# One PSUM bank for all turned probabilities of the cross heads in a decoder layer on one Trainium2 core

## Chip, cores, metric

The kernel runs on one core of a Trainium2 chip. The metric is the device time of one execution in microseconds (us). The profile is one execution taken by the hardware profiler.

## What is computed

One decoder layer on x of 8 x 256 tokens x 256 channels, float32, with three blocks, each followed by a residual sum and a layer norm:

```
x = layernorm(x + self_attention(x))      # 16 heads, three branches mixed by a gate
x = layernorm(x + cross_attention(x, ctx))
x = layernorm(x + experts(x))             # 8 experts, 2 active, softmax over masked scores
```

The change is in the cross attention:

```
qm, km, vm = split_heads(q @ Wq.T + bq), split_heads(k @ Wk.T + bk), split_heads(v @ Wv.T + bv)
scores = einsum('bnlh,bnph->bnlp', qm, km) / sqrt(16)      # 16 heads of 16 channels, 256 x 256
scores = where(mask, scores, -1e8)
attn = softmax(scores, axis=-1)
out = einsum('bnlp,bnph->bnlh', attn, vm)                  # then merged and times Wo
```

## The kernel before

The attention stage works on the eight rows of the batch, one after another; the expert stage follows. Each engine has its own program, written out by hand, and semaphores tie them together. For a row i the order on every engine is: the last self heads of row i, the cross attention of row i (projections, then sixteen cross heads), and the first self heads of row i+1. Between these steps `interleave` (L154) puts the pieces of `front(i + 1)`, the projections, rotations and the selection of 64 keys of the next row, one piece after nearly each step. So a PE step of the cross heads is followed by products for the next row.

PSUM has eight banks: S0 to S3, T0, T1, O and X, each 128 partitions of 512 float32 numbers. `block_plan` (L170) lists in the order of the program which result goes to which bank. For each bank there is a pair of semaphores, full and free. `before(name, i)` is the count of the free semaphore at which the previous user of the bank has been read out, and PE waits for it ahead of the first write; `after` is the count once the result itself has been read out. If a result moves from one bank to another in the list, the waits on all engines move with it.

The cross heads, for rows 0 to 6, go by steps h = 0 to 19:

- PE (L1783 to L1840): in even steps the scores of heads h and h+1 (`scores_x`, to S0 and S1; products 32 rows deep, `ps_S<-kx_sb,qx_sb`, eight of them); then four transposes of the normalised probabilities of head h-3 (`turn_probs_x`, L1798 to L1806, `<-ident,pr`, L1804); in steps 7, 11, 15, 19 the products of four heads with the values (`values_x`, `ps_O<-pT_sb,vx`). In the last steps the first self heads of the next row come in.
- VectorE (L1358 to L1390): `scores_x` reads the scores of a head out of PSUM, adds the mask and keeps the maximum (L1365, two per head); `denominators` inverts the sums of the exponentials (L1246). In an even step it does scores h, denominators h-1, scores h+1, and only then `turn_probs_x`, the copy of a turned head out of PSUM (L1378), for the heads of `VECTOR_TURNS`: 1, 5, 9, 13, 14, 15.
- ScalarE (L939 to L970): the exponentials of head h (L946), and ahead of them in its step the copy of turned head h-3 (L958) for the other heads.
- POOL (L724): normalises the probabilities of head h-1 (L728), four slots in turn, and computes rotations for the next row (L668 to L678) in between.
- SP issues the moves of rotated queries and keys of the next row.

Before the change the turned probabilities of even heads 0 to 12 go to S0, between the scores of the even heads, and all others to T0. A wait of PE's holds back everything behind it in its program. The last row has a plan of its own (`late`): turned heads in T0 and T1 in turn, scores in four banks.

The functions `turn_probs_x` and `scores_x` on PE wait like this:

```
for h in (h0, h0 + 1):                                   # scores_x, even step
    turns, f, row_ = sx(i, h)
    pe.wait_ge(turns.free_sem(f), turns.before(f, row_))
pe.wait_ge(prob_sb.sem, prob_sb.at(i, NH + h + 1))       # turn_probs_x
pe.wait_ge(turns.free_sem(f), turns.before(f, row_))
```

Of the kernel before, what the change touches and what calls it, by code (L numbers as in the profile page):

```python
# [19 lines left out]
NH = 16  # L20
# [149 lines left out]
def block_plan(full, free):  # L170

    plan = BankPlan(full, free)
    for h in range(NH):
        for half in range(2):
            if h >= HEAD_START:
                plan.add(("s", h, half), f"S{2 * (h % 2) + half}")
        for half in range(2):
            plan.add(("pT", h, half), f"T{half}")
    for g in range(4):
        plan.add(("o", g), ("X", "O")[g % 2])  # L180
    plan.add("proj", "S0")
    plan.add("ctxT", "O")
    plan.add("kx", "S0")
    plan.add("vx", "S1")
    plan.add("x1T", "T0")
    plan.add("qx", "O")
    for k in range(NH + 3):
        if k < NH and k % 2 == 0:
            plan.add(("sx", k), "S0")
            plan.add(("sx", k + 1), "S1")  # L190
        if k >= 3:
            h = k - 3
            plan.add(("pxT", h), "S0" if h % 2 == 0 and k < NH else "T0")
    for g in range(2):
        plan.add(("ox", g), "O")
    plan.add("projx", "O")


    for n, name in enumerate((
# [5 lines left out]
        plan.add(name, FRONT_BANKS[n % len(FRONT_BANKS)], ahead=True)  # L205
    for n, name in enumerate((("ksT", 0), ("ksT", 1))):
        plan.add(name, ("X", "T1")[n % 2], ahead=True)
    for h in range(HEAD_START):
        for half in range(2):
            plan.add(("s", h, half), f"S{2 * (h % 2) + half}", ahead=True)  # L210
    return plan
# [81 lines left out]
def attention_stage(nc, outer, block, sh, w):  # L293

    ctx = ExitStack()
    with ctx:
# [6 lines left out]
        BANKS = ("S0", "S1", "S2", "S3", "T0", "T1", "O", "X")  # L303
        pst = {b: ctx.enter_context(nc.psum_tensor(f"ps_{b}", [P, 512], F32)) for b in BANKS}
        plan = block_plan({b: sem(f"full_{b}") for b in BANKS}, {b: sem(f"free_{b}") for b in BANKS})

        def ps(name):
# [2328 lines left out]
```

## Time and profile before

| | |
|---|---|
| median of 3 runs | 1662.67 us (1662.43 to 1663.26) |
| the profiled execution | 1661.11 us |
| its span, first to last instruction | 1659.4 us |
| mean granted TensorE clock | 0.982 |
| PE busy | 1598.6 us, 96% |
| VectorE, ScalarE, POOL busy | 68%, 64%, 63% |
| attention stage | the first 975 us or so |

The profile names an instruction by its line, engine, operation, and out<-in tiles. A line of the timeline has its start, its length, and, in square brackets, the idle time of the engine ahead of it with what ended it. PE's matmuls overlap: a matmul's length is from its start to its modelled end, and the next one starts before that end. Where several of one kind follow each other they are merged (x4).

### The profile page before, as it was taken

The page shows a single profiled execution, that of the slowest core. Times are in us where ns is not written, and L with a number is a line of the kernel's source. Part 1 is how long each engine was busy: PE and PEld are TensorE (multiplying, and loading weights), DVE is VectorE, ACT ScalarE, POOL GpSimd, SP SyncE. Part 2 cuts the span into 40 slices and gives each one's busy share as a digit, 9 for nine tenths or more (in the row PEclk, how much of TensorE's full clock was granted, in tenths as well). Part 3 has the DMA queues.
Part 4 walks back from the last instruction along what each step waited for, and adds up shares of the span by engine and source line. Part 5 has one row for each costly group of instructions (what it writes and reads, how often), then busy time and mean ns, then how long its engine had stood idle before and what let it go on. Part 6 is the DMA issues. An engine that isn't in the chain of part 4 may idle for free.

```text
span 1659.4 us, 31027 instructions
## 1 busy us (share of the span) xinstructions
PE 1598.6 (96%) x9793; PEld 1251.9 (75%) x9793; DVE 1126.3 (68%) x3867; ACT 1058.0 (64%) x3165; POOL 1041.8 (63%) x1514
## 2 busy tenths in 40 slices
PE   6899999999999999999999899999999999999997
PEld 5577686786776776776867668888888888888886
DVE  4668768776877776687678546656565656666567
ACT  1575866946948847758579664556565666665652
POOL 2465665846747746657558474667675757575753
PEclk9899999999999999999999999999999999999998
DMA  7203103013012021031030110010101010101001
GB/s 223 69 2 78 27 2 93 11 29 76 2 45 60 2 60 44 2 77 27 12 87 2 53 52 27 18 60 18 68 16 64 14 64 14 64 13 64 13 1 51
DMA packets 54899, 70.77 MB, mean 43 GB/s; under 512 B 12688, under 2 KB 40976, under 8 KB 54736
## 3 DMA queue, kind: packets, MB, share of 16 engines
q1 hardware_dynamic: 54016, 66.04, 13.9%
q10 hardware_dynamic: 720, 2.75, 0.5%
q8 instruction: 79, 1.29, 0.3%
q14 instruction: 84, 0.69, 0.1%
HBM read 37.23 MB, written 2.16 MB: 24 GB/s over the span
## 4 chain that ended last, share of the span: by engine, by line
PE 78%; POOL 6%; issue 5%; ACT 5%; DVE 5%; DVEq 0%; POOLq 0%; ACTq 0%
PE ps_Y L2397 21%; PE ps_H L2397 19%; PE ps_S L1455 18%; PE ps_O L1455 5%; PE ps_T L1684 5%; PE ps_X L1455 5%; ACT pr L892 5%; POOL pr L728 3%; PE ps_T L1455 2%; PE ps_T L1804 2%; POOL rot L668 1%; PE ps_S L1804 1%; DVE sm L1365 1%; POOL rot L678 1%; POOL rot L674 1%
## 5 line engine op out<-in xcount | busy, mean ns | idle before, releaser
L2092 POOL TENSOR_TENSOR h_lo<-h_sb,h_hi 128x512 fp32r<-128x512 f32 x256 | 337.1, 1337 | 207.7 <-ACT h_sb L2135 207.3
L693 POOL TENSOR_TENSOR pr<-pr,rden 128x128 f32<-128x128 f32 (+2 forms) x768 | 307.9, 437 | 84.2 <-DVE rden L1246 83.8
L892 ACT ACTIVATE pr<-sm,nmx 128x128 f32<-128x128 f32 (+2 forms) x768 | 311.7, 413 | 22.4 <-DVE nmx L1257 22.4
L2134 ACT ACTIVATE h_hi<-h_sb,b_sb 128x512 fp32r<-128x512 f32 x224 | 160.6, 717 | 183.1 <-DVE h_sb L2318 183.1
L2318 DVE TENSOR_TENSOR h_sb<-ps_H,part 128x512 f32<-128x512 f32 x168 | 115.6, 688 | 211.6 <-PE ps_H L2397 200.5
L728 POOL TENSOR_TENSOR pr<-pr,rden 128x256 f32<-128x256 f32 x256 | 151.0, 618 | 116.3 <-DVE rden L1246 116.0
L1257 DVE CUSTOM_DVE_ANT_0 sm<-ps_S,cmask 128x128 f32<-128x128 f32 (+2 forms) x768 | 192.6, 308 | 33.5 <-PE ps_S L1455 24.6
L2397 PE MATMUL ps_Y<-h_hi,w_hi 128*128 128x512 f32 x512 | 199.7, 390 | 0.0
L2397 PE MATMUL ps_Y<-h_hi,w_lo 128*128 128x512 f32 x512 | 199.2, 389 | 0.0
L2397 PE MATMUL ps_Y<-h_lo,w_hi 128*128 128x512 f32 x512 | 199.2, 389 | 0.0
L2135 ACT ACTIVATE h_sb<-h_sb,b_sb 128x512 f32<-128x512 f32 x224 | 158.9, 709 | 0.0
L946 ACT ACTIVATE pr<-sm,nmx 128x256 f32<-128x256 f32 x256 | 127.9, 502 | 47.7 <-DVE nmx L1365 47.5
L892 ACT ACTIVATION_READ_ACCUMULATOR pr<-sm,nmx 128x1 f32 x768 | 148.9, 194 | 0.0
L1365 DVE CUSTOM_DVE_ANT_0 sm<-ps_S,sm 128x256 f32<-128x256 f32 x256 | 96.6, 417 | 53.8 <-issue 38.1
L1455 PE MATMUL ps_S<-kT_sb,qT_sb 96*128 96x320 f32 (+1 forms) x512 | 133.0, 382 | 0.0
L1684 PE MATMUL ps_T<-ident,pr 128*128 128x128 f32 x896 | 120.7, 275 | 10.8 <-DVE rot L1273 3.5
L1455 PE MATMUL ps_S<-latT_sb,qT_sb 128*128 128x128 f32 (+1 forms) x512 | 129.3, 335 | 0.9 <-DVE kT_sb L1235 0.9
L1684 PEld LDWEIGHTS ps_T<-ident,pr 128*128 128x128 f32 x896 | 100.8, 140 | 37.2 <-issue 23.3
L2397 PEld LDWEIGHTS ps_Y<-h_hi,w_lo 128*128 128x128 f32 x512 | 96.1, 188 | 20.0
L2397 PEld LDWEIGHTS ps_Y<-h_hi,w_hi 128*128 128x128 f32 x512 | 96.1, 188 | 20.0
L2397 PEld LDWEIGHTS ps_Y<-h_lo,w_hi 128*128 128x128 f32 x512 | 96.1, 188 | 19.8
L1455 PEld LDWEIGHTS ps_S<-kT_sb,qT_sb 96*128 96x128 f32 x512 | 88.0, 192 | 21.0 <-issue 0.6
(304 smaller groups left out, 3634.9 us busy)
## 6 DMA issues: line engine op xcount, KB each, us to landing
qT_sb<-rot SPq DMA_DIRECT2D x256, 64.0 KB, 2.0
w_raw<-in_W SPq DMA_DIRECT2D x16, 1024.0 KB, 6.7
kT_sb<-rot SPq DMA_DIRECT2D x192, 64.0 KB, 2.0
share<-shares SPq DMA_DIRECT2D x16, 512.0 KB, 3.7
xin<-in_x SPq DMA_DIRECT2D x8, 256.0 KB, 2.7
cin<-in_ctx SPq DMA_DIRECT2D x8, 256.0 KB, 2.7
w_kw<-in_wink ACTq DMA_DIRECT2D x2, 768.0 KB, 5.7
w_ks<-in_selk SPq DMA_DIRECT2D x2, 768.0 KB, 5.5
```

Source lines behind the costliest of these rows:

```text
L693: last = pool.tensor_tensor(p_, p_, rden[:, h % 2, n:n + 1].to_broadcast([P, width]), ALU.mult)
L728: last = pool.tensor_tensor(p_, p_, rden[:, h % 2, q:q + 1].to_broadcast([P, T]), ALU.mult)
L892: last = act.activation(pr[:, h % PR_SLOTS, a:a + width], sm[:, h % 2, a:a + width], ACT.Exp, bias=nmx[:, h % 2, n:n + 1], scale=-1.0, acc ...
L946: last = act.activation(prx[:, h % PR_SLOTS, T * q:T * q + T], smx[:, h % 2, T * q:T * q + T], ACT.Exp, bias=nmx[:, h % 2, q:q + 1], scale ...
L1257: ins = dve.tensor_tensor_reduce(out=sm[:, h % 2, a:a + width], in0=ps(f)[:, off:off + width], in1=cmask[:, m:m + width], scale=-ATT_SCALE ...
L1455: return pe.matmul(out, lhsT, rhs, start=start, stop=stop)
L1684: last = pe.transpose(ps(f)[:, dst:dst + P], p[:, a:a + P], ident[:, :])
L2092: pool.tensor_tensor(h_lo[:, g % RING, k, :], h_sb[:, k, :], h_hi[:, g % RING, k, :].bitcast(F32), ALU.subtract).then_inc(low_sb, 1)
L2134: act.activation(h_hi[:, g % RING, k, :], src, ACT.Relu, bias=bias)
L2135: act.activation(h_sb[:, k, :], src, ACT.Relu, bias=bias).then_inc(rect_sb, 1)
L2318: dve.tensor_tensor(out_, a, b, ALU.add).then_inc(sum_out, 1)
L2397: return pe.matmul(out_, lhsT, rhs, start=start, stop=stop)
```

## The change

In rows 0 to 6 the turned probabilities of all sixteen cross heads go to bank T0. S0 and S1 hold, in this stretch, the scores alone. The number and order of instructions are as before on each engine; the semaphores and counts that they wait for and raise follow from the list.

```
@@ -190,7 +190,7 @@
             plan.add(("sx", k + 1), "S1")
         if k >= 3:
             h = k - 3
-            plan.add(("pxT", h), "S0" if h % 2 == 0 and k < NH else "T0")
+            plan.add(("pxT", h), "T0")
     for g in range(2):
         plan.add(("ox", g), "O")
     plan.add("projx", "O")
```

## Rows read from the trace of the kernel before

**Rows 1.** The page, busy time of each engine over the span.
```profile
PE 1598.6 (96%) x9793; PEld 1251.9 (75%) x9793; DVE 1126.3 (68%) x3867; ACT 1058.0 (64%) x3165; POOL 1041.8 (63%) x1514
```

**Rows 2.** Two batch rows: us, PE, PEld, DVE, ACT, POOL busy, PEclk, DMA share, GB/s.
```profile
369.34:486.96 117.62, 114.78 (x844) 86.47 (x843) 86.40 (x401) 81.24 (x313) 73.46 (x144) 0.97 0.15 38
486.96:601.32 114.36, 111.53 (x843) 84.54 (x842) 86.48 (x401) 81.04 (x313) 73.55 (x144) 1.00 0.16 39
```

**Rows 3.** Same view, the same blocks of a long and of a short row.
```profile
394.50:401.30 6.80, 6.80 (x42) 4.71 (x41) 1.89 (x11) 3.79 (x12) 3.52 (x6) 0.50 0.40 96
512.20:519.00 6.80, 6.80 (x58) 4.00 (x56) 4.33 (x22) 5.29 (x17) 4.68 (x8) 1.00 0.34 82
```

**Rows 4.** Timeline of PE in the cross heads of row 3.
```profile
498.80 0.60 PE L1804 MATMUL ps_S<-ident,pr 128*128 128x128 f32 x4
499.23 1.89 PE L1455 MATMUL ps_S<-latT_sb,w_qd 96*128 96x256 f32 x8
501.27 1.13 PE L1455 MATMUL ps_S<-kx_sb,qx_sb 32*128 32x256 f32 x8
502.34 0.66 PE L1804 MATMUL ps_T<-ident,pr 128*128 128x128 f32 x4
503.64 0.66 PE L1804 MATMUL ps_S<-ident,pr 128*128 128x128 f32 x4 [0.65 <-POOL pr L728]
...
506.20 1.03 PE L1455 MATMUL ps_T<-latT_sb,w_qd 96*128 96x256 f32 x4
507.15 1.13 PE L1455 MATMUL ps_S<-kx_sb,qx_sb 32*128 32x256 f32 x8
...
509.38 0.63 PE L1804 MATMUL ps_S<-ident,pr 128*128 128x128 f32 x4
...
511.99 0.66 PE L1804 MATMUL ps_T<-ident,pr 128*128 128x128 f32 x4
...
513.42 0.66 PE L1804 MATMUL ps_S<-ident,pr 128*128 128x128 f32 x4
...
516.66 1.94 PE L1455 MATMUL ps_S<-w_ks,lat 128*64 128x512 f32 x8
...
523.21 0.63 PE L1804 MATMUL ps_S<-ident,pr 128*128 128x128 f32 x4 [0.51 <-DVE nmx L1365]
523.87 1.07 PE L1455 MATMUL ps_O<-pT_sb,vx 128*32 128x256 f32 x16
...
524.97 0.62 PE L1511 MATMUL ps_X<-ident,rot 64*96 64x64 f32 x8
525.70 0.62 PE L1511 MATMUL ps_T<-ident,rot 64*96 64x64 f32 x8
526.75 0.66 PE L1804 MATMUL ps_T<-ident,pr 128*128 128x128 f32 x4 [0.43 <-POOL pr L728]
527.26 0.46 PE L1455 MATMUL ps_S<-latT_sb,qT_sb 128*128 128x128 f32 x2
```

**Rows 5.** Timeline of VectorE (DVE) in the same heads.
```profile
499.29 0.68 DVE L1378 COPY pT_sb<-ps_T 128x512 f32<-128x512 f32 x1
...
508.46 0.42 DVE L1365 CUSTOM_DVE_ANT_0 sm<-ps_S,sm 128x256 f32<-128x256 f32 x1 [1.92 <-issue]
...
509.90 0.69 DVE L1378 COPY pT_sb<-ps_T 128x512 f32<-128x512 f32 x1
...
522.98 0.08 DVE L1365 DVE_READ_ACCUMULATOR2_ANT nmx<- 128x1 f32 x1
...
526.36 0.69 DVE L1235 COPY kT_sb<-ps_T 96x512 f32<-96x512 f32 x1 [1.32 <-PE ps_T L1511]
```

**Rows 6.** Timeline of ScalarE (ACT), copies of turned heads 3 and 11.
```profile
503.03 0.59 ACT L958 COPY pT_sb<-ps_T 128x512 f32<-128x512 f32 x1 [0.87 <-PE ps_T L1804]
...
523.14 0.59 ACT L958 COPY pT_sb<-ps_T 128x512 f32<-128x512 f32 x1
```

**Rows 7.** Timeline of POOL, normalisations of the last cross heads.
```profile
525.51 3.47 POOL L728 TENSOR_TENSOR pr<-pr,rden 128x256 f32<-128x256 f32 x6
```

More of the change, by code:

```diff
@@ L192, in block_plan @@
             h = k - 3
-            plan.add(("pxT", h), "S0" if h % 2 == 0 and k < NH else "T0")
+            plan.add(("pxT", h), "T0")
     for g in range(2):
```

## Prediction

> **What bounds the kernel.** Read first the busy times [rows 1]: PE is busy for 96% of the span, every other engine for at most 68%. A busy PE is not PE at its peak, so the next view is the stretch of one row of the batch, measured from its first cross scores to those of the next row [rows 2]. There are two kinds: 117.62 us and 114.36 us. The batch rows starting at 137.16, 369.34 and 601.32 are of the long kind, those at 254.82, 486.96 and 718.76 of the short (each within 0.2 us of the row shown). The clock view [rows 3] tells them apart: in three rows the clock granted to TensorE is 0.50, that is 1.2 GHz, for 6.8 us, while the same blocks run at 1.00, 2.4 GHz, in the other four. The price of one such drop is 117.62 - 114.36 = 3.26 us here; the other two pairs give a little less, and I take 3.1.
>
> The third view is PE in order of time inside the cross heads of a short row [rows 4]. Here the reader should look at start times: PE takes its blocks in program order, and the next block nearly always starts where the last one's array time ends (four transposes: 499.23 - 498.80 = 0.43 us). So PE's order is the path, and what counts is where a block starts later than that. A line with ps_S and x4 from L1804 is an even head's turned probabilities. By the program there are seven in each of seven rows (heads 0 to 12), and these 49 blocks are what the change moves.
>
> **What the change does, and what it removes.** Same instructions, same durations; only which release each of these blocks waits for changes. (1) Scores of heads k, k+1 no longer wait until ScalarE has copied head k-4's probabilities out of S0. (2) The probabilities of even head h no longer wait for VectorE's reading of score h+2. Both sound large; the array shows what they were. The scores of heads 6 and 7 start at 501.27, after eight products from 499.23. Four such products take 0.86 us (506.20 to 507.15 with the usual 0.09 of entry to the next scores), so eight end at 500.96 and the idle is 0.31, of which 0.22 is the wait for S0. The other scores of the row start within 0.1 us of the end of the block ahead, or behind a narrow product whose own tail is 0.2 to 0.3. Gain: **0.22 us a row**, at least 0 and, if all such tails were waits, at most 0.7.
>
> **What it adds.** Head h's four transposes now wait until head h-1 has been copied out of T0. I take 0.15 us from the end of a copy to the first transpose, because the read-out of the scores that ended at 523.06 [rows 5] released the transposes of 523.21 [rows 4]; 0.05 and 0.25 as ends. Working through the short row, heads in order:
>
> Head 2: VectorE copies head 1 only after the scores of heads 4 and 5, at 499.29 for 0.68 [rows 5]. Head 2 can start at 499.29 + 0.68 + 0.15 = 500.12 in place of 498.80: +1.32. VectorE was working without a break there, so its copy does not move. The scores of heads 6 and 7 then start at 500.12 + 0.43 + 1.73 + 0.09 = 502.37: +1.10, and head 3 at 503.44.
>
> Head 4: it waited for POOL at 503.64, and now for ScalarE's copy of head 3. That copy starts 503.03 - 502.34 = 0.69 after the first transpose and takes 0.59 [rows 6]: 503.44 + 0.69 + 0.59 + 0.15 = 504.87, a lag of 1.23.
>
> Head 6: scores 8 and 9 and VectorE behind them lag 1.23 (VectorE had been waiting for them: it starts on them at 508.46 [rows 5], after PE's 507.15). Its copy of head 5 comes behind both scores again: 509.90 + 1.23 + 0.69 + 0.15 = 511.97 against 509.38. Lag 2.59.
>
> Head 8: 511.99 + 2.59 + 0.69 + 0.59 + 0.15 = 516.01 against 513.42. Lag 2.59, and all up to the selected keys' products at 516.66 carries it.
>
> Head 12: ScalarE's copy of head 11 ends at 523.14 + 0.59 = 523.73 [rows 6], so head 12 starts at 523.88 in place of 523.21, 0.67 more (head 10 adds a little at most and I leave it out). Not all survives: head 13 at 526.75 waits for POOL, whose work runs on from the rotated selected keys into the next normalisations at 525.51 [rows 7], and this follows the lag of 516.66 only. But the two groups of selected keys are turned 1.10 and 1.83 us after the values' products (524.97 and 525.70 against 523.87), and VectorE's copy of the second (526.36, [rows 5]) releases the next row's first scores at 527.26. Both distances hold a wait for POOL, whose time doesn't move with head 12, so part of the 0.67 goes into it: I estimate that 0.26 does and 0.41 stays (ends 0 and 0.67).
>
> Sum per row 2.59 + 0.41 = **3.0 us**, seven rows 21.0. By the ends of the 0.15 (in four steps) and of the 0.41 a row costs 2.2 to 3.7. Heads 13 to 15 were in T0 before; the last row keeps its own plan; the expert stage and every DMA are untouched, at nothing. SP issues the same moves in the same order, released by POOL and ScalarE; PE asks for them only ahead of the next row's scores, and with PE later they have more time. POOL's queue and ScalarE's keep their order; behind ScalarE's later copy of head 2 stand only exponentials that wait for scores which lag as much.
>
> **The clock.** Ahead of each of the three drops stand the same blocks: head 5, three position products one column wide, head 6, a product 32 rows deep, scores 32 rows deep, head 7 (around 509.38 [rows 4]; the drops [rows 3]). Four rows pass this place at full clock, three do not, so it is at the edge. The change puts 1.36 us more idle into just this place. I expect the drop in all seven: four more, 4 x 3.1 = 12.4 us. The ends are three drops fewer and, since the idle before head 2 is new too, seven more.
>
> The Trainium skill (TensorE: Matmul & The Clock Gate, "A second HAM failure mode: psum-queue depth-cycling") says that short idles of PE between groups, from cycling through PSUM banks, can make the clock swing between its two levels; the trace agrees that this place swings, and by that rule the 12.4 stands.
>
> Profiled execution: 1661.11 (span 1659.4 and 1.7 around it). 1661.11 + 21.0 + 12.4 = 1694.5. The median of the runs is 1.56 above the profiled one: **1696 us**.
>
> The starts in [rows 4] also say that separating scores from probabilities frees hardly any array time, because front products of the next row already cover it. The Trainium skill (Perfetto Trace Analysis, "Optimizing Tensor Performance", Matmuls) wants independent groups to rotate through different PSUM banks, so that one's evacuation overlaps the next group. It speaks against this change, which takes the second bank from the transposes, and for it in what it does to the scores; the rows above price the first at 3.2 a row, the second at 0.22. By the rule alone there would be a loss without a size.
>
> **Rivals.** (a) Waits as worked out, clock as before: 1662.67 + 21.0 = 1684. For it: four rows do pass that place at full clock, and the drops may hang on the moment rather than on the idle. Chance 0.20. (b) More drops: the idle before head 2 or around head 12 brings a second one to each row, up to 7 x 3.1 more: 1706 to 1718. Against it: those places have wide products close by. 0.08. (c) One of the two long waits is hidden, because VectorE gets to head 1 or 5 sooner when its neighbours lag: 7 x 1.3 = 9 less than forecast or than (a), 1672 to 1687. 0.09. (d) Both are hidden, POOL's normalisation sets the pace, no change: 1660 to 1666. VectorE's copies would have to end 1.3 us earlier, and the first [rows 5] has no idle ahead of it. 0.08. (e) **Faster.** Mechanism: S0 free of copies lets scores go out early, so VectorE, waiting for the scores of head 8 (1.92 us idle ahead of 508.46 [rows 5]), runs ahead and finishes head h-1's copy before PE wants T0. Price: 0.22 at the scores, 0.22 before head 12, 7 x 0.44 = 3.1, and the three clock drops saved, 9.3: 1650. It decides at head 2: VectorE must be done with head 1 by 498.65; it is done at 499.97, held by its own work and not by scores. 0.05.
>
> **Numbers.** Forecast 0.50. The range leaves out (d), (e), half of (b) and a little of (c): 1676 to 1709. A measurement of this kernel can tell about 0.2% (3.3 us) from no change. Faster 0.05, same 0.08, slower 0.87.
>
> **What would show it.** In the profile after: ps_T with all 512 turned blocks' records of cross heads, none to ps_S; PE idle before even heads put down to VectorE's copy (line 1378) some 14 times with about 1.3 us, and to ScalarE's (line 958) at heads 4, 8 and 12; head 2 starts 0.15 us after the end of VectorE's copy of head 1, in place of 1.17 us before it. Rows 117.5 us without a drop and 120.6 with one; clock 0.50 in seven stretches. The forecast is wrong if head 2 still starts ahead of that copy's end, if rows of the short kind stay at 114.4, or if the waits are there and the clock drops in three rows or fewer.

## The result and the profile after

The changed kernel takes 1698.99 us (median of 4 runs, 1698.08 to 1703.56) beside 1662.55 for the kernel before in the same comparison (4 runs, 1655.21 to 1663.26). The ratio is 1.0259, with an interval of 1.0229 to 1.0289: slower by 2.6%. The forecast was 1696 and its range 1676 to 1709. The profiled execution took 1699.47 us, its span is 1697.8, the mean granted clock 0.971; before they were 1661.11, 1659.4 and 0.982.

The page of the changed kernel, busy times and the two slice lines of PE:

```profile
PE 1615.4 (95%) x9793; PEld 1261.5 (74%) x9793; DVE 1126.2 (66%) x3867; ACT 1060.7 (62%) x3165; POOL 1042.4 (61%) x1514
...
PE   6899999998998999999999989999999999999997
PEclk9899999998999998999998999999999999999998
```

Beside [rows 1]: the busy times of VectorE, ScalarE and POOL are within 3 us, and PE's grew by 17 us with the same 9793 instructions. An instruction count that stands still while busy time grows points to the clock; the rest of the 38.4 us by which the span grew must be idle. The same windows as [rows 2], for six rows of the batch, and then the longest and two common clock drops, a drop being a stretch at 0.50 (columns: us, PE, PEld, DVE, ACT, POOL busy, PEclk, DMA share, GB/s):

```profile
137.92:259.89 121.97, 116.30 (x843) 87.31 (x842) 86.38 (x401) 81.55 (x313) 73.58 (x144) 0.96 0.14 35
259.89:380.06 120.17, 114.54 (x843) 86.52 (x842) 86.54 (x401) 81.36 (x313) 73.61 (x144) 0.97 0.15 37
380.06:502.05 121.99, 116.35 (x844) 87.45 (x843) 86.44 (x401) 81.59 (x313) 73.58 (x144) 0.96 0.15 37
502.05:622.19 120.14, 114.52 (x843) 86.55 (x843) 86.53 (x401) 81.45 (x313) 73.58 (x144) 0.97 0.15 37
622.19:743.92 121.73, 116.01 (x843) 87.28 (x842) 86.55 (x401) 81.60 (x313) 73.66 (x144) 0.96 0.15 36
743.92:864.19 120.27, 114.38 (x843) 86.37 (x842) 86.70 (x401) 81.47 (x313) 73.55 (x144) 0.97 0.15 37
...
890.30:904.00 13.70, 13.70 (x63) 7.71 (x59) 4.27 (x22) 7.00 (x22) 4.74 (x8) 0.50 0.30 74
405.60:415.80 10.20, 10.20 (x51) 6.89 (x52) 2.50 (x14) 5.78 (x17) 3.64 (x7) 0.50 0.40 98
528.50:535.30 6.80, 6.80 (x39) 4.77 (x35) 1.98 (x11) 4.13 (x14) 3.46 (x6) 0.50 0.38 91
```

No row has a clock of 1.00 any more. Every row of the seven has a drop at heads 5 to 7, 6.8 us long in four, 10.2 in two and 13.7 in the seventh (864.19 to 980.89, 116.7 us beside 107.8 before); the fifth row has a second one of 3.4, at 665.0. That is 64.7 us at 0.50 beside 3 x 6.8 = 20.4 before.

The timeline of PE in row 3, which begins at 502.05 here and at 486.96 before, so that 15.09 is to be taken off for a comparison with [rows 4]:

```profile
513.02 1.03 PE L1455 MATMUL ps_T<-latT_sb,w_qd 96*128 96x256 f32 x4
515.20 0.63 PE L1804 MATMUL ps_T<-ident,pr 128*128 128x128 f32 x4 [1.14 <-DVE pT_sb L1378]
515.66 1.89 PE L1455 MATMUL ps_S<-latT_sb,w_qd 96*128 96x256 f32 x8
517.48 1.13 PE L1455 MATMUL ps_S<-kx_sb,qx_sb 32*128 32x256 f32 x8
518.54 0.66 PE L1804 MATMUL ps_T<-ident,pr 128*128 128x128 f32 x4
519.97 0.63 PE L1804 MATMUL ps_T<-ident,pr 128*128 128x128 f32 x4 [0.77 <-ACT pT_sb L958]
...
524.51 0.66 PE L1804 MATMUL ps_T<-ident,pr 128*128 128x128 f32 x4
...
525.37 0.36 PE L1455 MATMUL ps_S<-marks,upper 128*128 128x1 f32 x2
527.03 0.63 PE L1804 MATMUL ps_T<-ident,pr 128*128 128x128 f32 x4 [1.30 <-DVE pT_sb L1378]
527.59 0.69 PE L1455 MATMUL ps_S<-w_qd,latT_sb 32*128 32x512 f32 x1
...
530.42 1.12 PE L1804 MATMUL ps_T<-ident,pr 128*128 128x128 f32 x4
```

The two copies of VectorE that these waits name, and, from the list of the line of the transposes, its count and the waits ahead of it:

```profile
514.37 0.68 DVE L1378 COPY pT_sb<-ps_T 128x512 f32<-128x512 f32 x1
...
526.19 0.69 DVE L1378 COPY pT_sb<-ps_T 128x512 f32<-128x512 f32 x1
```

```profile
L1804 PE MATMUL ps_T<-ident,pr x512: 271/273/476, 144.2 to 1014.2; 128*128 128x128 f32 x171
...
  DVE pT_sb L1378: 17.1, 14
  ACT pT_sb L958: 13.5, 14
```

514.37 + 0.68 + 0.15 = 515.20: PE stands with head 2 until VectorE has copied head 1. 526.19 + 0.69 + 0.15 = 527.03: the same at head 6 behind the copy of head 5. Seven rows give 14 waits of 1.2 us on average (longest 1.3) on VectorE, and 14 of 1.0 (longest 1.2) on ScalarE, at heads 4 and 12. Neither kind was there before. In this row the clock falls at 528.5, behind the one-column products, the wait, head 6 and the product 32 rows deep: at 530.42 four transposes span 1.12 us, where the usual is 0.66.

### The profile page after: what moved, and what is told of

Same layout as the page of the kernel before. It is cut to its first block, busy times and chain, and to the rows that moved or that the text cites. A ratio compares the mean times of both kernels' runs of the same rounds, so it can differ in the third digit from the quotient of the medians.

```text
span 1697.8 us, 31027 instructions
## 1 busy us (share of the span) xinstructions
PE 1615.4 (95%) x9793; PEld 1261.5 (74%) x9793; DVE 1126.2 (66%) x3867; ACT 1060.7 (62%) x3165; POOL 1042.4 (61%) x1514
## 3 DMA queue, kind: packets, MB, share of 16 engines
q1 hardware_dynamic: 54016, 66.04, 13.7%
## 4 chain that ended last, share of the span: by engine, by line
PE 80%; ACT 6%; issue 6%; DVE 5%; POOL 3%; DMA 0%; DVEq 0%; POOLq 0%; ACTq 0%
PE ps_Y L2397 21%; PE ps_S L1455 20%; PE ps_H L2397 18%; ACT pr L892 5%; PE ps_O L1455 5%; PE ps_T L1684 4%; PE ps_X L1455 4%; PE ps_T L1804 3%; PE ps_T L1455 3%; POOL pr L728 1%; DVE sm L1365 1%; DVE pT_sb L1378 1%; DVE rt L1083 1%; POOL rot L678 1%; POOL rot L668 1%
## 5 line engine op out<-in xcount | busy, mean ns | idle before, releaser
L1684 PE MATMUL ps_T<-ident,pr 128*128 128x128 f32 x896 | 120.6, 274 | 10.8 <-DVE rot L1273 3.5
L1684 PEld LDWEIGHTS ps_T<-ident,pr 128*128 128x128 f32 x896 | 100.9, 140 | 37.2 <-issue 23.4
L1804 PE MATMUL ps_T<-ident,pr 128*128 128x128 f32 x512 | 89.1, 302 | 34.6 <-DVE pT_sb L1378 17.1
L1804 PEld LDWEIGHTS ps_T<-ident,pr 128*128 128x128 f32 x512 | 61.5, 153 | 75.1 <-issue 42.6
```

The lines of the kernel that those rows point to most:

```text
L1684: last = pe.transpose(ps(f)[:, dst:dst + P], p[:, a:a + P], ident[:, :])
L1804: last = pe.transpose(pst[turns.bank(f)][:, T * k + P * q:T * k + P * q + P], prx[:, h % PR_SLOTS, T * q + P * k:T * q + P * k + P], ident ...
```

## The experiments

The theory had two parts: waits of PE at heads 2, 6 (VectorE), 4 and 12 (ScalarE), and a clock drop that the wait at head 6 brings about. The experiments take these apart. Their ratios are to the kernel before in runs beside them (1658.3, 1658.9, 1657.2 and 1654.8 us in the four groups of runs, each between 1649.9 and 1665.8).

**Half of the change each.** First, only heads 2 and 6 go to T0, then only the other five (both edits are against the changed kernel):

```
-            plan.add(("pxT", h), "T0")
+            plan.add(("pxT", h), "S0" if h % 2 == 0 and k < NH and h not in (2, 6) else "T0")
```

> Of the even heads only 2 and 6 go to T0, the five others stay in S0. Theory (PE waits for VectorE's copies of heads 1 and 5, which stand behind two heads' scores, and the longer idle makes the clock drop in every row): the two waits of 1.3 us each remain, less 0.22 for the freed scores and a little that head 4 absorbs, 2.3 us a row or 16, and the clock falls in all seven rows, 12 to 17 more: 1690 us, range 1684 to 1696. Rival (the loss lies in the one bank as such, spread over all seven heads): two sevenths of 36 us, 1673.

```
-            plan.add(("pxT", h), "T0")
+            plan.add(("pxT", h), "S0" if h in (2, 6) else "T0")
```

> The reverse: heads 2 and 6 stay in S0, the five others go to T0. Theory: head 4 costs 0.13, head 10 0.13, head 12 0.67 of which 0.4 stays, the rest nothing: 0.6 us a row or 4, and the clock falls in three rows as before: 1667 us, range 1660 to 1672, so that the two halves of the change don't share the loss evenly. Rival (one bank as such): five sevenths of 36 us, 1689.

Two heads: 1693.13 us, ratio 1.0208 (1.0175 to 1.0241). Five heads: 1661.17 us, 1.0022 (0.9999 to 1.0045). The row with the shortest drop in the first, and the first row of the second kernel, which has none (the same windows):

```profile
499.04:617.16 118.12, 113.14 (x844) 86.00 (x843) 86.48 (x401) 81.34 (x313) 73.63 (x144) 0.99 0.15 37
```

```profile
137.99:252.94 114.95, 111.57 (x843) 84.34 (x842) 86.29 (x401) 81.03 (x313) 73.51 (x144) 1.00 0.15 37
```

Two of the seven moved heads carry nearly the whole loss, and they are those behind VectorE's copies. The other five cost some 0.4 us a row (rows without a drop take 114.75 to 114.95, in the kernel before 114.4 to 114.5). In the first kernel the clock is at 0.50 for 54.4 us of the seven rows, in the second for 10.2. So it is the waits at heads 2 and 6 that bring the further drops; no run here has one of the two without the other at its full length and the blocks around it unchanged, so the part of the wait at head 6 alone is argued from where the clock falls.

**The copy in between.** In the changed kernel, VectorE takes the copies of heads 1, 5 and 9 between the two scores of its step instead of behind both; every head stays in T0:

```
+                    ahead = following is not None and h - 3 in (1, 5, 9)
+                    if ahead:
+                        turn_probs_x(h - 3)
                     if h < NH and h % 2 == 0:
                         scores_x(h + 1)
-                    if 3 <= h < NH + 3:
+                    if 3 <= h < NH + 3 and not ahead:
```

> The changed kernel with VectorE's copies of turned heads 1, 5 and 9 put ahead of the second head's scores in its step, no longer behind both. Theory (the wait is VectorE's copy standing behind the scores): heads 2 and 6 start 0.7 us sooner each, 1.4 us a row; a row without a drop of the clock comes to 115.9 us (114.4 in the kernel before, 117.3 in the changed one), and with some drops left 1680 us, range 1670 to 1688. Rival (the copy follows the transposes whatever its place, or scores read later cost as much as is won): rows as changed, 1695 or more.

1682.83 us, 1.015 (1.012 to 1.018). Its one row without a drop, and PE at heads 2, 4 and 6 of that row:

```profile
376.18:491.93 115.75, 111.53 (x845) 84.59 (x844) 86.45 (x401) 81.14 (x313) 73.57 (x144) 1.00 0.15 39
```

```profile
388.63 0.63 PE L1807 MATMUL ps_T<-ident,pr 128*128 128x128 f32 x4 [0.46 <-DVE pT_sb L1378]
...
393.40 0.63 PE L1807 MATMUL ps_T<-ident,pr 128*128 128x128 f32 x4 [0.77 <-ACT pT_sb L958]
...
399.78 0.63 PE L1807 MATMUL ps_T<-ident,pr 128*128 128x128 f32 x4 [0.61 <-DVE pT_sb L1378]
```

The waits at heads 2 and 6 shrink by 0.68 and 0.69 us, a head's reading of scores on VectorE, and the wait at head 4 stays: what PE waits for is the place of the copy in VectorE's order. The drops stay in the other six rows (47.6 us).

**ScalarE copies heads 1 and 5.** The changed kernel with one list altered:

```
-VECTOR_TURNS = (1, 5, 9, 13, 14, 15)
+VECTOR_TURNS = (9, 13, 14, 15)
```

> The changed kernel with the copies of turned heads 1 and 5 given to ScalarE, which idles there; all heads still in T0. Theory (the loss is who copies, and behind what, not the one bank): head 2 doesn't wait, head 6 by 0.3 us, head 12 as in the changed kernel; a row without a drop 115.0 us, 1662 us in all, range 1655 to 1668, no more drops than in the kernel before. Rival (one bank for neighbouring heads costs a full hand-over of 1.4 us each time): 1680 or more.

1661.77 us, 1.0021 (1.0002 to 1.004). A row without a drop, and PE at heads 2 and 4 in it:

```profile
252.65:367.65 115.00, 111.45 (x844) 84.58 (x843) 84.97 (x399) 82.20 (x315) 73.47 (x144) 1.00 0.16 39
```

```profile
264.49 0.60 PE L1804 MATMUL ps_T<-ident,pr 128*128 128x128 f32 x4
...
269.31 0.66 PE L1804 MATMUL ps_T<-ident,pr 128*128 128x128 f32 x4 [0.84 <-POOL pr L728]
```

Head 2 has no idle ahead of it, head 4 waits for POOL as before, and head 6 still waits 0.20 us for ScalarE, in place of 1.30 for VectorE. With all heads in one bank a row costs 0.4 to 0.5 us over before, and the ratio falls from 1.0259 to 1.0021: the bank alone is nearly free, the release behind VectorE's queue is not. The kernel before with the same two copies on ScalarE was not run, so what the lighter VectorE gives by itself is not taken apart.

**The clock by itself.** The product behind head 6 is 32 rows deep. It is made 128 rows deep, in the changed kernel and in the one before, with the same columns. The product then multiplies by query weights as well, so that its values are not those of the layer: these two kernels serve for timing alone.

```
-                    product(i, ("v1", t), P, HW, [latT[QK:P, 1, P * t:P * t + P]], [w_dv[QK:P, :]])
+                    low = 0 if t == 0 else QK
+                    product(i, ("v1", t), P, HW, [latT[low:P, 1, P * t:P * t + P]], [w_dv[low:P, :]])
```

> The changed kernel with the first latent value product of each row run over all 128 rows of the array in place of 32, in the same time (it then multiplies by query weights as well, so these values are others than the reference's). No wait differs. Theory (the drops of the clock come from the little work that the array does around head 6): the granted clock stays at full there in most rows and the drops' share goes, 1699 - 25 = 1674 us, range 1670 to 1682; what stays above the kernel before with the same edit is the waits alone, 21 us. Rival (the longer rows have another cause, and the clock only goes with it, or falls for other reasons): 1697 or more.

> The kernel before with the same edit of the first latent value product (its values are others than the reference's). Theory: no drop of the clock in the seven rows, three times 3.1 us less: 1653 us, range 1651 to 1656. Rival: 1662, drops in three rows as before.

The changed kernel with it: 1683.52 us, 1.0147 (1.012 to 1.0174), a little more than its range allowed. The kernel before with it: 1651.53 us, 0.9965 (0.9944 to 0.9986), as expected. From head 6 to the scores behind the product it takes the same time at full clock, 1.55 us with the shallow product (kernel before) and 1.54 with the deep one:

```profile
391.75 0.63 PE L1804 MATMUL ps_S<-ident,pr 128*128 128x128 f32 x4
392.30 1.12 PE L1455 MATMUL ps_S<-w_qd,latT_sb 32*128 32x512 f32 x2
393.30 1.13 PE L1455 MATMUL ps_S<-kx_sb,qx_sb 32*128 32x256 f32 x8
```

```profile
389.10 0.63 PE L1805 MATMUL ps_S<-ident,pr 128*128 128x128 f32 x4
389.56 1.02 PE L1455 MATMUL ps_S<-w_qd,latT_sb 128*128 128x512 f32 x2
390.64 1.13 PE L1455 MATMUL ps_S<-kx_sb,qx_sb 32*128 32x256 f32 x8
```

Two rows of the changed kernel with the deep product and two of the kernel before with it:

```profile
137.18:254.46 117.28, 111.61 (x844) 84.14 (x843) 86.29 (x401) 81.24 (x313) 73.62 (x144) 1.00 0.15 36
491.95:609.01 117.06, 111.44 (x844) 84.25 (x844) 86.45 (x401) 81.24 (x313) 73.58 (x144) 1.00 0.15 38
```

```profile
137.59:252.21 114.62, 111.67 (x843) 84.42 (x842) 86.38 (x401) 81.06 (x313) 73.51 (x144) 1.00 0.15 37
...
481.26:595.60 114.34, 111.47 (x844) 84.53 (x843) 86.52 (x401) 81.06 (x313) 73.52 (x144) 1.00 0.16 39
```

This gives the waits a price free of the clock. Three rows of each kernel can be put side by side: 117.28 - 114.62, 117.06 - 114.34 and 117.22 - 114.52 are 2.66, 2.72 and 2.70 us. It also shows the drop to be a matter of its own: in the kernel before, with one deeper product, none of the seven rows has one. That is the profiled execution; of the others the mean granted clock speaks, .988 to .991 in all nine runs, while ten of the 18 of the kernel before beside them lie below .988. In the changed kernel, with its idle ahead of head 6, it is not enough: three rows still drop there (at 279.7, 634.7 and 873.6), and three short drops come in elsewhere, 27.2 us together beside 64.7. At 3.1 us for 6.8 that is some 12 us, more than the miss. Its row at 491.95 shows the end of the chain of waits too:

```profile
529.54 0.66 PE L1805 MATMUL ps_T<-ident,pr 128*128 128x128 f32 x4
531.36 0.63 PE L1805 MATMUL ps_T<-ident,pr 128*128 128x128 f32 x4 [1.16 <-ACT pT_sb L958]
```

From head 11 to head 12 it is 1.82 us; before it was 523.21 - 522.05 = 1.16 us in row 3.

**More work at the drop.** In the kernel before, two products of 128 rows and 256 columns fill the place ahead of the shallow one; in a second kernel head 1 is copied by ScalarE too, and head 2 is in T0:

```
+                    if t == 0:
+                        pe.wait_ge(plan.free_sem(("v1", t)), plan.before(("v1", t), i))
+                        for _ in range(2):
+                            mm(ps(("v1", t))[:, 0:T], ident[:, :], latT[:, 1, :])
...
-VECTOR_TURNS = (1, 5, 9, 13, 14, 15)
+VECTOR_TURNS = (5, 9, 13, 14, 15)
...
-            plan.add(("pxT", h), "S0" if h % 2 == 0 and k < NH else "T0")
+            plan.add(("pxT", h), "S0" if h % 2 == 0 and k < NH and h != 2 else "T0")
```

> The kernel before with two more products, 128 rows deep and 256 columns wide, into the bank of the first latent value product ahead of it, whose own first product overwrites them: the output is unchanged, PE has 0.43 us more work a row. Theory (the array's little work there makes the clock drop): no drops in the seven rows, rows of 114.9 us, 1654 us with a small spread, against 1650 to 1663 of the kernel before. Rival (added work is only added, drops stay): 1661 with the same spread.

> The same, and ScalarE copies head 1, with head 2 in T0, so that the scores of heads 6 and 7 no longer wait for S0. Theory: 0.2 us a row less than without it, 1652.5 us. Rival: the earlier copy delays ScalarE's exponentials and nothing is won, 1654 or more.

1657.52 us, 0.9993 (0.9975 to 1.0011), and 1658.06 us, 0.9996 (0.998 to 1.0012), where 1654 and 1652.5 were expected. The drops did leave the seven rows of both profiled executions. But a row takes 115.0 to 115.4 us instead of 114.4, 0.3 more than I had reckoned for the two products, and the last row, which has none of these products in it, has a drop of 23.9 us in the first kernel's trace, where the kernel before has one of 13.7. The second kernel wins nothing further: with S0 free the scores of heads 6 and 7 come 0.2 us sooner, but head 4 then waits 0.88 us for POOL instead of 0.65. Filling the place with added work costs what it saves; the deeper product costs no time.

**Full products between heads 5 and 6.** PE's piece with the last two query products (96 rows deep, 256 columns, 1.7 us) changes places with the one-column position products. So the query products now stand between heads 5 and 6 and the position products go ahead of the scores of heads 8 and 9, while the product 32 rows deep stays where it was, behind head 6; ScalarE's readings move by a piece. Its core, on PE, in the kernel before, the changed one, and the changed one with ScalarE's copies:

```
-                queries(1, 0)
-                queries(1, 3)
-                yield
...
+                yield
+
+                queries(1, 0)
+                queries(1, 3)
```

> The kernel before with two pieces of the next row's projections exchanged on PE (the last two query products, 1.7 us at full depth, come after head 5 and the three position products ahead of them; ScalarE's copies of them move along). Theory: the array works hard just where it had little to do, the clock stays at full in the seven rows, rows of 114.4 us, 1651 us with a small spread. Rival: ScalarE's later copies hold up its exponentials and POOL, PE waits for head 8, rows 1 us longer, 1657 or more.

> The changed kernel with the same exchange. Theory (PE's wait for T0 at head 6 is idle because nothing stands between heads 5 and 6; work there covers it, and head 2's wait stays): the wait at head 6 falls from 1.36 to 0.3 us, a row without a drop 116.2 us, and with a few drops left at other places 1667 us, range 1661 to 1676. Rival (the waits only move on): 1690 or more.

> The exchange together with all heads in T0 and ScalarE copying heads 1 and 5. Theory: no long wait and no drop, rows of 114.9 us, 1654 us with a small spread: one bank costs next to nothing once neither copy nor clock stands against it. Rival: ScalarE, with two copies more and the moved ones, becomes late, 1660 or more.

On the kernel before 1654.96 us, 0.9991 (0.9974 to 1.0008); on the changed one 1669.99, 1.0089 (1.0058 to 1.0119); with ScalarE's copies 1660.36, 1.0026 (1.0006 to 1.0047). A row of the second, and PE at head 6 in the next row:

```profile
257.91:373.89 115.98, 111.47 (x843) 84.49 (x842) 86.89 (x401) 81.09 (x313) 73.57 (x144) 1.00 0.16 39
```

```profile
395.79 1.03 PE L1455 MATMUL ps_X<-latT_sb,w_qd 96*128 96x256 f32 x4
396.65 1.03 PE L1455 MATMUL ps_T<-latT_sb,w_qd 96*128 96x256 f32 x4
397.81 0.63 PE L1804 MATMUL ps_T<-ident,pr 128*128 128x128 f32 x4
398.36 0.69 PE L1455 MATMUL ps_S<-w_qd,latT_sb 32*128 32x512 f32 x1
```

The second has the whole change in it, its wait at head 2 too, and no drop in any of the seven rows of its profiled execution. It takes 29 us less than the changed kernel, 7 of them by shorter waits (seven times 2.7 less 1.7), the rest by the clock. That execution was its fastest (1666.22 us, clock .989); the other three are at 1669.7 to 1670.6 and .985 to .987, so their rows may not all have been free of drops. Now eight products of known length (four ahead of 396.65, four behind it, 0.86 us each) stand ahead of head 6 and not three narrow ones: the idle there is 397.81 - 396.65 - 0.86 = 0.30 us where it was 1.30, so a row costs 1.7 over the 114.4 of the first kernel. The exchange changes two things at once, this idle and the blocks beside it; in the first kernel, which had no such idle, the blocks alone do it. That one missed its expected 1651 us though its rows were as expected, because the exchange in the ramp before the first row brings a drop of 13.7 us there (the first cross scores come at 140.5, before at 137.2). The third missed its 1654 as well: drops appear at 179.1, 756.0 and 872.0, none of which I foresaw.

**The exchange in the later rows alone.** The same exchange on the kernel before, for all rows but the first, whose products stand in the ramp (PE's side of it):

```
-                queries(1, 0)
-                queries(1, 3)
-                yield
+                if i == 0:
+                    queries(1, 0)
+                    queries(1, 3)
+                    yield
...
+                if i:
+                    queries(1, 0)
+                    queries(1, 3)
+                    yield
```

> The kernel before with the exchange in the seven interleaved fronts only, the first front (which nothing is interleaved with) as it was. Theory: e9's first cross scores came at 140.5 us in place of 137.2, because a drop of the clock in the first front lasted longer; with that front as before the 3.3 us are won back: rows of 114.4 us and 1651.5 us, at most 1654, faster than the kernel before by 0.3 to 0.5%. Rival: the first stage's drops vary from run to run by themselves, 1655 as e9.

1652.74 us (1650.53 to 1656.92, 12 runs), 0.998 (0.9962 to 0.9998): within the expected time, but 0.2% faster and not 0.3 to 0.5%, and that only just clear of no change. Two of its rows:

```profile
252.36:366.64 114.28, 111.35 (x843) 84.68 (x842) 86.75 (x401) 80.89 (x313) 73.50 (x144) 1.00 0.16 39
481.02:595.34 114.32, 111.38 (x843) 84.56 (x842) 86.73 (x401) 80.86 (x313) 73.50 (x144) 1.00 0.16 39
```

The first six rows have no drop (114.2 to 114.6 us); the seventh has one of 3.4. The kernel before took 1651.64 to 1665.76 in the 17 runs beside it, so that the fastest runs of the two differ by 1 us and the slowest by 9: what is won is mostly that the long times are missing.

## Why the prediction was right

It was right in direction, mechanism and range, 3 us short of the median. Part of that closeness is luck: against the profiled execution the waits were 2.1 us too large and the clock's term 7.8 too small, and the 1.56 us from the profiled time to the median was added on, where the changed kernel's median lies 0.5 below. The 3 drops of the kernel before were taken as given, too; its later runs spread from 1649.9 to 1665.8 us.

- **The gain** of S0 free of copies. The scores of heads 6 and 7 start at 517.48 - 15.09 = 502.39, the forecast was 502.37. From the eight products ahead of them it is 517.48 - 515.66 = 1.82 us and was 501.27 - 499.23 = 2.04: the 0.22 of the working.
- **Head 2** starts at 515.20 - 15.09 = 500.11, forecast 500.12. **Head 4**: 519.97 - 15.09 = 504.88, forecast 504.87. **Head 6**: 527.03 - 15.09 = 511.94, forecast 511.97. The 0.15 us from a copy's end to the first transpose, taken from one place of the trace, held at both copies of VectorE. ScalarE's waits show at heads 4 and 12, 14 times; the one foretold for head 8 is there by the start times (head 8 comes 1.42 us after head 7, 520.84 - 519.42 in the row at 491.95), but the profile puts no idle to it.
- **Head 12** waits 0.66 us longer than before from head 11, forecast 0.67.
- **The sum of the waits** was 3.0 us a row and measured 2.7, so 7 x 2.7 = 18.9 and not 21.0. Two things were mis-sized. The lag of head 6 is as forecast (2.56 for 2.59), but it was taken to reach the selected keys whole, and there it is 2.40: their products start 524.05 - 491.95 = 32.10 us after the row's first scores (changed kernel with the deep product), before 516.66 - 486.96 = 29.70. From head 6 to head 7 it takes 519.42 - 516.93 = 2.49 us, before 511.99 - 509.38 = 2.61. And of head 12's 0.67, 0.41 was to stay: the first products of the next self heads start at 534.95 - 491.95 = 43.00 us after the row's first scores, before at 527.26 - 486.96 = 40.30, so 2.70 - 2.40 = 0.30 stays.
- **The clock.** Forecast: a drop in all seven rows, 3.1 us each, so four more, 12.4 us. There is one in all seven rows at the place named, but three of them are longer than any seen there before, and the fifth row has a second one. 64.7 - 20.4 = 44.3 us more at half clock, at 3.1 us for 6.8, are 20.2 us. This is the term that was too small: the number of drops was counted and their length taken for granted. Rows of 120.6 us were forecast; three are within 0.5 of that, three are 1.1 to 1.4 above it, and the seventh is 8.9 above its own former 107.8, where 6.1 was forecast.
- **The sum** then reads, against the profiled spans: 18.9 + 20.2, plus 0.8 ahead of the first row and less 1.4 behind the last row's first scores, 38.5; measured 1697.8 - 1659.4 = 38.4.

The rivals. (a) Waits with the clock as before, 1684: the waits were right, the clock was not. (b) A second drop in each row: one row has one. For the rest the time beyond the forecast comes from longer drops, which (b) did not name; its 1706 was not reached. (c) and (d), one or both waits hidden: both stand, 14 times. (e), faster through an early copy: head 2 is released at 514.37 + 0.68, after PE wants it, as the working said; VectorE was held by its own work.

On the Trainium skill (TensorE: Matmul & The Clock Gate, "A second HAM failure mode: psum-queue depth-cycling"): the place did swing as that rule says of short idles between groups. But idle is not the whole of it here: the kernel before, with no idle added and one deep product, lost its drops. On the Trainium skill (Perfetto Trace Analysis, "Optimizing Tensor Performance", Matmuls): the rule to rotate banks pointed the right way for the change, though with ScalarE's copies a single bank costs 0.4 to 0.5 us a row and not 2.7.

What stays open is why the drops are of 6.8 us in one row and 10.2 or 13.7 in another with the same blocks in it. The traces show one regularity: in the first six rows of the changed kernel the drops that start 25.4 and 25.6 us after the row's first scores last 10.2, those that start at 25.8 to 26.9 last 6.8 (the second, short one of the fifth row apart); with heads 2 and 6 alone in T0, 10.2 belongs to starts at 24.5 to 25.8, 6.8 to 26.0 to 26.9 and 3.4 to 27.3. What sets the start is not shown. The new places of the kernels with ScalarE's copies are not scattered either: four of their five drops start 37.0 to 37.3 us after the row's first scores, where head 12 (at 36.9 to 37.1) now waits 1.2 us for ScalarE, which is the place that rival (b) named. That this wait brings them on was not tested.

## What to carry to other kernels

Before a result is moved to a bank, look at who empties the bank's previous result and what stands ahead of that copy in its engine's order: a copy behind two heads' readings of scores cost PE 1.1 to 1.3 us each time, the same copy on another engine nothing at head 2 and 0.2 at head 6. Where a trace shows the clock falling at one place in some rows and not in others, count that place as fragile, and price idle put there at a whole drop in every row, or more: 64.7 us of drops came of 20.4 here. First try another order of the pieces: full products between the narrow ones cost nothing in a row here (114.2 to 114.6 us) and steadied the times from run to run. Added work cost what it saved. A deeper product cost no time, but the two kernels that had one computed other values; whether rows of zeros would do the same was not run.

## What the runs showed of the hardware

The depth of one product can go with whether the clock falls. In the kernel before, making the one product behind head 6 128 rows deep in place of 32, at the same columns, took the drops out of all seven rows, 1651.5 us for 1658.3. It is not this depth alone: with the product left 32 rows deep at its place, and query products put between heads 5 and 6 where the one-column products had stood, the seven rows of the profiled execution had no drop either. Where 1.3 us of idle stands ahead of head 6, as in the changed kernel, the depth alone took out a little over half of the drop time (27.2 us left of 64.7); the exchange, which also cuts this idle to 0.3, took out all of it in the profiled execution. The Trainium skill (TensorE: Matmul & The Clock Gate, "What's actually happening") says that the clock follows how busy PE has been; by the busy time alone the two kernels would hardly differ (111.53 us of PE in a row at full clock [rows 2], 111.47 with the deep product), and they do.

The spread of 1650 to 1664 us for an unchanged kernel goes largely with the clock as well. Of its 70 runs in the first three groups, 19 had a mean granted clock of .981 to .983 and a median of 1662.3 us, 17 one of .990 or .991 and a median of 1651.3; the 34 between them lie at .984 to .989 and 1651.8 to 1663.6 us, so the mean clock does not settle a time by itself. The changed kernel's four runs lie at .968 to .972.
